# Silu as one function in a second activation table, a fourth state on GpSimd, and small scales in PSUM, in a two-direction state-space block with a quantised linear layer

## The reference, cut to what matters

```python
def _mamba(x, win, wconv, bconv, wx, wdt, bdt, Alog, Dp, wout):
    xz = x @ win.T
    u, z = jnp.split(xz, 2, axis=-1)                  # 1024 columns each
    u = silu(causal_conv_of_4(u, wconv) + bconv)
    dbc = u @ wx.T                                    # dt (32), B (16), C (16)
    delta = softplus(dt @ wdt.T + bdt)
    dA = exp(delta[..., None] * A)
    dBu = (delta * u)[..., None] * B[:, :, None, :]
    # step over t: h = dA_t * h + dBu_t ; y_t = sum_n h[n] * C_t[n]
    y = y + u * Dp
    y = y * silu(z)
    return y @ wout.T

scales = max(max(abs(block)) / 7.5, 1e-30)
q = nearest_on_grid(block / scales)
```

## Time and profile before

| | |
|---|---|
| median of 3 runs | 7830.91 us (7823.11 to 7831.89) |
| profiled execution, its own time | 7834.85 us |
| its span, first to last instruction | 7832.9 us |
| VectorE busy | 7360.3 us, 94% |
| GpSimd busy | 7301.4 us, 93% |
| TensorE busy | 6926.4 us, 88% |
| ScalarE busy | 5962.0 us, 76% |
| granted TensorE clock, mean | 0.960 |

### The profile page before, as it was taken

One profiled execution on the slowest core, in us unless ns is written; L12 is line 12 of the kernel. 1 busy time (PEld: TensorE's weight loads), 2 busy tenths in 40 slices (PEclk: granted clock), 3 DMA queues, 4 the chain that ended last, 5 costly groups with the idle time before them and its releaser, 6 DMA issues. The chain is left out here.

```text
span 7832.9 us, 140448 instructions
## 1 busy us (share of the span) xinstructions
PE 6926.4 (88%) x32680; PEld 4049.9 (52%) x32680; DVE 7360.3 (94%) x11770; ACT 5962.0 (76%) x12302; POOL 7301.4 (93%) x4074
## 2 busy tenths in 40 slices
PE   6899988999888988999889889989889899899788
PEld 3455545555555555555555555555555555555444
DVE  0799999999999999999999999999999999999698
ACT  1777778888777878888787878878778887777544
POOL 1899999999999999999999999999999999999577
PEclk8999999999999999999999999999999999999999
DMA  5444445444444444354444543444444444444544
GB/s 161 144 133 130 126 133 146 125 117 140 133 128 127 131 143 135 108 145 130 129 130 123 146 145 100 142 134 133 124 124 142 144 119 123 135 133 130 176 150 145
DMA packets 597342, 1049.46 MB, mean 134 GB/s; under 512 B 113456, under 2 KB 221872, under 8 KB 588016
## 3 DMA queue, kind: packets, MB, share of 16 engines
q1 hardware_dynamic: 594384, 1038.78, 44.9%
q10 hardware_dynamic: 2080, 1.05, 0.0%
HBM read 909.69 MB, written 129.91 MB: 133 GB/s over the span
## 5 line engine op out<-in xcount | busy, mean ns | idle before, releaser
L622 POOL TENSOR_TENSOR dBu<-Bb,du 128x1024 f32<-128x1024 f32 x2048 | 4801.7, 2364 | 50.8 <-DVE h L1155 24.3
L771 ACT ACTIVATE dA<-delta,A 128x512 f32<-128x512 f32 x4096 | 2831.9, 699 | 828.6 <-DVE h L1155 391.4
L1155 DVE TENSOR_TENSOR_SCAN h<-dA,state,dBu 128x512 f32<-128x512 f32 x2048 | 2641.3, 1290 | 230.2 <-ACT dA L771 194.2
L993 PE MATMUL yT<-ident,hC 128*128 128x128 f32 x10240 | 1590.5, 284 | 378.4 <-DVE hC L1171 358.2
L993 PEld LDWEIGHTS yT<-ident,hC 128*128 128x128 f32 x10240 | 1196.2, 144 | 901.0 <-DVE hC L1171 570.5
L1171 DVE TENSOR_TENSOR hC<-h,Cb 128x512 f32<-128x512 f32 x2048 | 1393.8, 681 | 0.0
L631 POOL TENSOR_TENSOR hR<-hR,Cb 128x512 f32<-128x512 f32 x768 | 978.6, 1274 | 71.2 <-DVE state L1184 51.0
L986 PE MATMUL bg<-u,comb 128*128 128x512 f32 x2112 | 996.0, 595 | 2.5 <-ACT pre L733 1.1
L1155 DVE TENSOR_TENSOR_SCAN hV<-dA,state,dBu 128x512 f32<-128x512 f32 x768 | 969.0, 1262 | 21.6 <-ACT dA L771 11.8
L925 PE MATMUL bg<-hT,win_u 128*128 128x512 f32 x2112 | 968.7, 599 | 0.9 <-ACT hT L666 0.9
L1155 DVE TENSOR_TENSOR_SCAN hR<-dA,state,dBu 128x512 f32<-128x512 f32 x768 | 966.5, 1258 | 2.8 <-ACT dA L771 2.8
(11 more groups left out here) (163 smaller groups left out, 9384.4 us busy)
## 6 DMA issues: line engine op xcount, KB each, us to landing
comb<-pre_scratch SPq DMA_DIRECT2D x1040, 256.0 KB, 4.5
Bb<-bc_scratch SPq DMA_DIRECT2D x264, 512.0 KB, 8.3
Cb<-bc_scratch SPq DMA_DIRECT2D x264, 512.0 KB, 7.5
win_u<-in_win SPq DMA_DIRECT2D x264, 256.0 KB, 4.2
pre_scratch<-pre SPq DMA_DIRECT2D x264, 256.0 KB, 3.2
comb<-comb_scratch SPq DMA_DIRECT2D x66, 1024.0 KB, 7.1
win_z<-in_win SPq DMA_DIRECT2D x257, 256.0 KB, 2.7
part_scratch<-pre SPq DMA_DIRECT2D x132, 256.0 KB, 2.0
```

What stands on the lines that cost most here:

```text
L622: pool.tensor_tensor(dBu[:, q % AHEAD], Bb[:, 2 * q:2 * q + 2, :], du[:, j % 2, :].unsqueeze(1).broadcast_to([P, 2, T]), ALU.mult).then_in ...
L771: act.activation(dA[dA_bank(v, j, n)][:], delta[:, j % 2, :], ACT.Exp, scale=A[:, v % 2, j * N + n:j * N + n + 1]).then_inc(dA_made, 1)
L993: ins = nc.tensor.matmul(yT[:, tt * P:(tt + 1) * P], product[:, tt * P:(tt + 1) * P], ident[:], start=first and tt == 0, stop=False, is_tr ...
L1155: nc.vector.tensor_tensor_scan(to, dA[dA_bank(v, j, n)][:], dBu[:, q % AHEAD, k, :], state[:, c:c + 1], ALU.mult, ALU.add).then_inc(h_made, 1)
```

## The change

- silu(u) and silu(z) become one ScalarE function, Silu, which lives in another activation table. At seven steps of a chunk (`GATED`), at the end of the step, ScalarE loads that table, runs Silu in place over two tiles (1024 columns) of u or z or both, and loads the first table back. z gets two buffers. GpSimd's `finish_u` and `finish_z` go. In the prologue one Silu runs over all eight tiles of u.
- State 4 joins `ASIDE`. With 4 and 5 both aside, pair 2 has no product on VectorE. hR gets a fourth buffer.
- The steps of some Z, U, X, K, D0 and H change, and X is taken two steps after its last piece instead of one.
- Last stage: `f_amax`, the reciprocals and a copy of the scales (`own`) move to PSUM; the two products with broadcast constants become one scalar operation with two constants, run once into PSUM and once into SBUF; `f_po` has one bank for each of two tiles instead of two, and `finish` runs in halves.

```diff
-ASIDE = (3, 7, 11)
+ASIDE = (3, 4, 7, 11)
-HC, HR, HV = 4, 3, 2
+HC, HR, HV = 4, 4, 2
...
-    ("D2", (7,), 1), ("Z1", (9, 10), 1), ("O2", (11, 11, 12, 12, 13, 13, 14, 14), 0), ("D3", (15,), 1),
+    ("O1", (6, 6, 7, 7, 9, 9, 10, 10), 0), ("D2", (7,), 1), ("O2", (11, 11, 12, 12, 13, 13, 14, 14), 0), ("D3", (15,), 1),
...
-TAKE = {name: at[-1] + (2 if name[0] in "ZTUCD" else 1) for name, at, bank in SCHEDULE}
+TAKE = {name: at[-1] + (2 if name[0] in "ZTUCDX" else 1) for name, at, bank in SCHEDULE}
...
+GATED = {7: (("Z", 0),), 23: (("Z", 2),), 31: (("C", 0),), 39: (("C", 2), ("Z", 4)), 47: (("C", 4),), 51: (("C", 6),),
+         55: (("Z", 6),)}
...
-                        if 2 * q + 1 in ASIDE:
+                        if 2 * q in ASIDE or 2 * q + 1 in ASIDE:
                             sp.wait_ge(hR_made, aside(last, 2 * q + 2))
...
-                    if p == 3:
+                    if p == 1:
                         sp.wait_ge(bg_ready, ready(i, "Y7"))
                         load_z(d, 1)
...
-                            if q == 1:
-                                finish_z(g - 1)
...
-                            for m in range(MT):
-                                if p == TAKE[f"C{m}"] + (5 if m < MT - 1 else 4):
-                                    finish_u(i + 1, 1 - s, m)
...
+            def silu_u(taken, m, count, s):
                 act.wait_ge(bg_free, taken)
+                both = u[:, s, m:m + count, :].rearrange("p m t -> p (m t)")
+                act.activation(both, both, ACT.Silu).then_inc(u_made, count)
+
+            def take_z(made, bank, j, before):
                 act.wait_ge(bg_ready, made)
+                act.wait_ge(gated, before)
+                act.copy(z[:, j % 2, :], bank[:]).then_inc(bg_free, 1)
+
+            def silu_z(taken):
                 act.wait_ge(bg_free, taken)
+                both = z[:].rearrange("p a t -> p (a t)")
+                act.activation(both, both, ACT.Silu).then_inc(z_made, 2)
...
+                            if p in GATED:
+                                nc.scalar.preload_act_table_set(SILU)
+                                for kind, m in GATED[p]:
+                                    if kind == "C":
+                                        silu_u(freed(i, f"C{m + 1}"), m, 2, 1 - s)
+                                    else:
+                                        silu_z(freed(i, f"Z{m + 1}"))
+                                nc.scalar.preload_act_table_set(EXP_LN)
...
+                            for n in pair:
+                                c = j * N + n
+                                if n in SIDE:
+                                    dve.wait_ge(h_made, g * N + n + 1 + H0)
+                                if n in ASIDE:
+                                    last = hR[:, (j * NA + ASIDE.index(n)) % HR, T - 1:T]
+                                    nc.vector.tensor_copy(state[:, c:c + 1], last).then_inc(side_saved, 1)
...
+        per = ps("f_per", [P, 3, 4 * NBLK])
+        amax, own, rscale = per[:, 0, :], per[:, 1, :], per[:, 2, :]
...
-                nc.vector.tensor_tensor(amax[:, 0:n], amax[:, 0:n], step_of[:].broadcast_to([P, n]),
-                                        ALU.mult).then_inc(step_made, 1)
-                dve.wait_ge(step_made, r + 1)
-                nc.vector.tensor_tensor(own, amax[:, 0:n], least[:].broadcast_to([P, n]), ALU.max).then_inc(scale_made, 1)
-                dve.wait_ge(scale_made, r + 1)
-                nc.vector.reciprocal(rscale[:, 0:n], own).then_inc(rscale_made, 1)
+                nc.vector.tensor_scalar(own[:, 0:n], amax[:, 0:n], GRID / FP6_MAX, GRID * 1e-30, ALU.mult,
+                                        ALU.max).then_inc(own_made, 1)
+                dve.wait_ge(own_made, r + 1)
+                nc.vector.reciprocal(rscale[:, 0:n], own[:, 0:n]).then_inc(rscale_made, 1)
+                nc.vector.tensor_scalar(scale[:, a % 2, 0:n], amax[:, 0:n], GRID / FP6_MAX, GRID * 1e-30, ALU.mult,
+                                        ALU.max).then_inc(scale_made, 1)
```

More of the change, by code:

```diff
@@ L98 @@
 NUM_ACT = {name: e for e, name in enumerate(BY_ACT)}
+GATED = {7: (("Z", 0),), 23: (("Z", 2),), 31: (("C", 0),), 39: (("C", 2), ("Z", 4)), 47: (("C", 4),), 51: (("C", 6),),
+         55: (("Z", 6),)}
+assert all(TAKE[f"{kind}{m + 1}"] <= p for p in GATED for kind, m in GATED[p])
+assert sorted(m for p in GATED for kind, m in GATED[p]) == sorted(2 * list(range(0, MT, 2)))
+assert all(m * NQ + NQ > p for p in GATED for kind, m in GATED[p] if kind == "Z")
 PROLOGUE = (["H0", "H1", "H2", "H3", "U0", "U1", "U2", "C0", "U3", "C1", "U4", "C2", "U5", "C3", "U6", "C4", "U7", "C5",
@@ L351, in scan_stage @@
         side = lambda g, n: g * (NA + NT) + len([k for k in SIDE if k < n])
+        KEEPING = [q for q in range(NQ) if 2 * q in STRAIGHT or 2 * q + 1 in STRAIGHT]
+        kept = lambda g, q: g * len(KEEPING) + len([k for k in KEEPING if k < q])
         IN_PLACE = [n for n in STRAIGHT if n % 2]
@@ L1159, in _ @@
                                 gate(ready(i, name), bg[OWN_BANK], g - 1, (j - 1) % MT, s if j else 1 - s)
-                            own = 2 if 2 * q + 1 in STRAIGHT else 1
-                            for k in range(own):
-                                n = 2 * q + k
+                            pair = (2 * q, 2 * q + 1)
+                            own = [n for n in pair if n in STRAIGHT]
+                            for n in own:
+                                c = j * N + n
                                 dve.wait_ge(h_made, g * N + n + 1 + H0)
-                                if own == 1:
-                                    nc.vector.tensor_copy(state[:, j * N + n:j * N + n + 1],
-                                                          h[:, T - 1:T]).then_inc(state_saved, 1)
+                                bank = dA[dA_bank(v, j, n)] if n in IN_PLACE else h
+                                if len(own) == 1:
+                                    nc.vector.tensor_copy(state[:, c:c + 1], bank[:, T - 1:T]).then_inc(state_saved, 1)
@@ L1167, in _ @@
                                 dve.wait_ge(hC_used, straight(g, n) - C0 + 1)
-                                if j == 0 and k == 0:
+                                if j == 0 and n == own[0]:
                                     dve.wait_ge(C_loaded[q], i * 16 + 16)
-                                bank = dA[dA_bank(v, j, n)] if n in IN_PLACE else h
                                 nc.vector.tensor_tensor(hC[:, (j * NS + STRAIGHT.index(n)) % HC, :], bank[:],
                                                         Cb[:, n, :], ALU.mult).then_inc(hC_made, 1)
-                                if k == 0:
+                                if n == pair[0]:
@@ L1174, in _ @@
                                     dve.wait_ge(h_made, g * N + n + 2 + H0)
-                                if k == 0 and own == 2:
-                                    nc.vector.tensor_copy(state[:, j * N + n:j * N + n + 1], h[:, T - 1:T])
-                                    nc.vector.tensor_copy(state[:, j * N + n + 1:j * N + n + 2],
+                                if n == pair[0] and len(own) == 2:
+                                    nc.vector.tensor_copy(state[:, c:c + 1], h[:, T - 1:T])
+                                    nc.vector.tensor_copy(state[:, c + 1:c + 2],
@@ L1535, in finish @@
             def finish(r, a, stores):
-                dve.wait_ge(ffn_mm, r + 1)
                 dve.wait_ge(bias_added, r + 1)
                 wait_past(dve, stored[a % 2], stores)
-                nc.vector.tensor_tensor(res[:, a % 2], po[:, a % 2], x1[:, a % SLOTS], ALU.add).then_inc(res_made, 1)
+                for t in range(2):
+                    dve.wait_ge(ffn_mm, 2 * r + (t + 1))
+                    nc.vector.tensor_tensor(res[:, a % 2, t], po[:, t], x1[:, a % SLOTS, t], ALU.add).then_inc(res_made, 1)
             def divide(r, a):
```

114 lines of the change are left out of this document (34 added, 80 removed), and 16 rows, old and new, of the table GENERAL.

## The result

| | before | after |
|---|---|---|
| median of 4 runs | 7829.45 us (7823.11 to 7831.89) | 8040.82 us (8028.39 to 8040.85) |
| ratio | | 1.0267, 95% interval 1.025 to 1.0285 |
| span of the profiled execution | 7832.9 us | 8026.5 us |
| first gate, last gate | 241.0, 7362.4 | 238.5, 7605.9 |
| last gate to the end of the span | 470.5 us | 420.6 us |

The forecast was 7765 us, with 7655 to 7855 as its range. The table splits the 193.6 us by which the span grew: 2.5 us gained ahead of the first gate, 49.9 us gained behind the last, and 246.0 us lost between them, in the scan stage. There a chunk takes (7605.9 - 238.5) / 32 = 230.2 us instead of 222.5. The profiled execution of after took 8028.39 us, 12 us less than its median; everything that is counted in chunks comes from profiled executions.

What follows compares the result with a forecast made beforehand. VectorE was taken to set the scan's pace, GpSimd just ahead. A chunk's -4.1 - 2.8 - 0.5 + 6.2 = -1.2 us gives -38 over 32; last stage -30, prologue +2.5: -66, so 7765 us, range 7655 to 7855.

Steps and rivals of the forecast that it cites:

- pair 2: States 4 and 5 of every tile lose their product with C: 3.14 to 2.62 us, saving 4.1 us a chunk.
- X, its wait for GpSimd: Once a chunk TensorE waits for GpSimd's last product of u with its sigmoid, delaying X and dA; 2.8 us gone.
- load, Silu of 1024: ScalarE's burst instructions: 1.30 us a table load, 1.07 us a Silu of 1024 columns, bounds 0.65 and 1.3.
- small waits: VectorE's other idle time, 1.4 us a chunk; 0.5 taken as gone because ScalarE loses six activations a tile.
- stalls at the bursts: VectorE stalls at seven ScalarE bursts a chunk, 0.1 to 2.4 us each, 6.2 us a chunk in sum.
- prologue: The eight tiles' Silu comes in one piece at the end, 4096 columns and two loads: +2.5 us once.
- last stage: VectorE operations that read PSUM get shorter, TensorE then bounds: pairs from 11.47 to 10.5 us, 30 us gained.
- ScalarE gets back ahead in the following pair: After a burst ScalarE recovers its lead since its other work became less; nothing was added for this.
- Priced at nothing: Moved Z loads and later C and B rows in SP's queue cost nothing; otherwise GpSimd waits 1 to 2 us a chunk.
- the third: TensorE enters the tile late after a burst, ScalarE waits for its banks: 2 to 3 us a chunk, 7830 to 7860; 17%.
- The second rival: Each of 14 table loads a chunk costs more than its row, slower; at twice the row 8340 us; 8%.
- The first rival: Bursts stay hidden from VectorE, a chunk falls by 7.4 us: 7566 us, 12%; half hidden 7665, 13%.

Runs made afterwards that it cites:

- half of the projections: The changed kernel with four matmuls cut to two for each u and z bank, bursts and loads kept: 7805.67 us, chunk 223.3.
- The run without loads: The changed kernel without table loads in the scan stage, Exp in place of Silu, so other values are computed: 7701.92 us, chunk 220.0.
- the one with X later: Before with the new last stage, X taken two steps after its last piece, K, D0, Z7 and H2 moved to make room: 7728.31 us, ratio 0.9882.
- T comes last: The changed kernel with TensorE doing the transposes of a turned state after the other pieces of the same step: 8001.64 us, chunk 229.4.

## Why the prediction was wrong

| term | predicted | measured | |
|---|---|---|---|
| pair 2 | -0.51 us a tile | 3.14 to 2.76: -0.38; pair 1 another -0.06 | right, a little large |
| X, its wait for GpSimd | -2.8 us a chunk | gone, -2.75 | right |
| load, Silu of 1024 | 1.30, 1.07 us | 1.283, 1.055 to 1.059 us | right |
| small waits | -0.5 us a chunk | about -0.4 (7.7 against 8.1 above) | right |
| stalls at the bursts | +6.2 us a chunk | +14.4, 1.57 of it where no burst is | **wrong** |
| prologue | +2.5 us | not seen (below) | wrong, small |
| last stage | -30 us | -49.9 us | right mechanism, too small |

**The step that failed** is the one that sized the stalls: "From that dA's start, which is the end of scan 12, to the next tile's first scan are 3017.03 - 3010.99 = 6.04 us". It is the end of scan 12 only if ScalarE is free at that moment. Of the 8.2 us by which the stalls exceed the forecast, steps 7, 23 and 55 hold 5.5, and there the dA ahead of the burst starts 0.5 to 2.7 us late; step 39 holds 0.7 (hist waits 0.63 us for TensorE within the burst), step 43 1.6. Two more judgements went with it. "ScalarE gets back ahead in the following pair [...] I add nothing" left out what ScalarE waits for in that pair. "Priced at nothing", on the moves, looked at the loads that Z1 to Z7 depend on and at SP's queue, and not at what TensorE and ScalarE do in the steps just before each burst. There the change itself makes the lateness: it puts Z1's eight matmuls into steps 4 and 5, among those of O0, and Z3's into steps 20 and 21, beside U0. State 15's dA at step 7 starts 0.46 us late in before and 2.28 in after, at step 23 0.24 and 2.73; with half of the projections it is 0.29 and 0.03, and with U0 one step earlier (and O3 closer together) 1.32 at step 23. No run undid the move at step 7 alone.

The trace of before could have told a part of it. ScalarE's waits for the banks of u and z were there (95.4 and 87.7 us, in rows that the prediction did not show), and VectorE felt little of them: dA of state 15 at step 39 starts 1.36 us late in every chunk of before, with no stall behind it. The finished dAs that stand between the two engines are a lead, and it was in use. The prediction spent this lead once, on the burst, and took it as full each time. The run without loads shows the lead absorbing nearly all of 412 us of waits; the run with half of the projections shows it absorbing most of the bursts; after asks both of it.

One smaller slip: GpSimd was to fall to about 95%. By the prediction's own 1.27 us of 27.8 a tile it falls from 97.8 to 93%; the 90.1% that was measured is of a longer tile.

**Of the rivals**, the third was nearest: "TensorE does not catch up", ScalarE waits for its banks. It was priced at 2 to 3 us a chunk as the aftermath of a burst. The stalls exceed the forecast by 8.2 us, and 5.5 of them come of lateness ahead of a burst. The low clock at step 43 is in no rival. The second rival, loads that cost more than their row, is out: in the rows of step 23 Silu ends at 3312.68 and the load back starts at 3312.70, ends at 3313.98, and dA starts at 3313.99. Over all 448 loads in the scan the gap is 17 to 19 ns ahead of a load and 11 to 12 ns behind it. The drain of about 1380 ns that the Trainium skill adds to each switch ("ScalarE: Activation LUTs", What ACT_TABLE_LOAD costs) is not seen here; the measurement decides. The first rival, hidden bursts, is out too.

**Last stage.** Rounds went from 11.47 us on average to 10.07 in the round above, not 10.5. TensorE is granted 1.00 there, where the sum took 0.97; but the round of 10.29 us from which it started had run at 1.00 too (7601.39 to 7611.68), so what the sum added to it was for low stretches of the clock, and after has none there (1.00 from 7715 to 8018). The last rounds are shorter, 8.3 us, and from the first finishing add (7712.5) to the first one of the last pair (8019.2) the average is 9.89: 31 x (11.47 - 9.89) = 49 us. Another 4 us are gained ahead of the first add (110.5 to 106.6 us behind the last gate) and 3 lost behind the last (4.4 to 7.3). f_ratio fell from 2.78 to 1.22 us with one input in PSUM, beyond what the sum counted on, but TensorE is the bound by then.

**Prologue.** The first gate comes 2.5 us earlier rather than later. That is hardly an effect of the change: with the old prologue it stands at 241.0 in before, at 239.5 in the run with the new last stage alone and at 235.6 in the one with X later, with the new one between 238.0 and 239.6 in the six kernels that have it, and at 239.1 in the one of them without loads. So the 2.5 us that the prediction added are not seen, and what the prologue is worth otherwise is within this spread.

**Open**: why the dA at step 7 is late by 1.6 us in most chunks and by 3.3 to 3.8 in the others, what delays TensorE when T comes last, and whether a table of steps exists with which after's bursts are entered on time. By the run with half of the projections such a table would give about 7806 us, so it would not beat the last stage alone.

## What to carry to other kernels

Buffers between two engines are one reserve, and every lateness of the producer is paid from it: before a block of work is put in front of a producer, add up what the producer waits for in the steps just ahead of it, even where the consumer shows no wait for it now. A wait that costs nothing in the profile is a sign that the reserve is in use there, not that it is free. And of a change in four parts, run the parts: here two of them are worth about 0.6% each, the fourth state aside is worth 3.8 us a chunk beside the bursts, and the loads cost more than all of them.

## What the runs showed of the hardware

- With a TensorE that was idle for 1.77 us at the same instruction of the same program, the eight matmuls behind it took 3.60 us in one chunk and 5.29 us in another: the granted clock over the 4 us was 1.00 in the one case and 0.57 in the other. It was low in 10 of the 32 chunks. In after, where the idle time at this place is 2.5 to 2.7 us, it was low in all 32, for 3.4 us in 13 and 6.8 us in 19.
- A table load and the activations around it follow each other without a gap: 1.283 us a load, 0.01 to 0.02 us on either side.
- A VectorE operation over 32 columns took 1.10 and 1.83 us on average with both inputs in SBUF, and 0.20 and 0.17 us with its input in PSUM; over 1024 columns 2.78 became 1.22 us. GpSimd was busy beside them for most of their time in both. The small operations also changed their form, but in before itself f_ratio, unchanged, took 1.22 us in a round where GpSimd ran nothing beside it and 3.04 in the next, where GpSimd's f_nrm ran until 7620.87:

```profile
7609.17 1.22 DVE L1557 TENSOR_TENSOR f_ratio<-f_nrm,f_rscale 128x1024 f32<-128x1024 f32 x1
...
7618.92 3.04 DVE L1557 TENSOR_TENSOR f_ratio<-f_nrm,f_rscale 128x1024 f32<-128x1024 f32 x1
```

The Trainium skill says that a VectorE instruction with two SBUF inputs contends with a GpSimd instruction that reads SBUF ("SBUF — State Buffer", Who interferes with whom), and the trace agrees.
